# Padding each slot of a weight buffer from 1025 to 1056 elements

## The reference

```python
qkv = xn @ attn_qkvw + attn_qkvb                      # 32 heads of 32
scores = einsum('bhqd,bhkd->bhqk', q, k) * hd ** -0.5
ctx = softmax(scores) @ v;  attn = ctx @ attn_ow + attn_ob

q = xn @ Wq_w.T;  scores = q @ keys.T                 # router, 64 experts
gate = softmax over the top 16 of 64, zero elsewhere
z = (xn @ A_w.T) * gate (each gate for 8 columns)     # 512 columns
out = (z @ B_w.T) * 2
```

## Time and profile before

| | us |
|---|---|
| three timed runs, median | 2559.98 |
| lowest and highest of them | 2558.9, 2560.48 |
| the profiled execution: its time | 2557.13 |
| the profiled execution: its span | 2555.3 |
| TensorE busy in the span | 2507.6 |
| VectorE, ScalarE, GpSimd busy | 1510.5, 1208.0, 1634.3 |

### The profile page before, as it was taken

The page is one execution under the profiler, slowest core; times in us unless marked ns, Lnnn a source line. Parts: engine busy times, 40 slices in busy tenths (PEclk is TensorE's granted clock), DMA queues, the critical chain, the costliest instruction groups (busy, mean ns, idle before and its releaser), DMA issues. The chain is left out here.

```text
span 2555.3 us, 34397 instructions
## 1 busy us (share of the span) xinstructions
PE 2507.6 (98%) x12888; PEld 1633.1 (64%) x12888; DVE 1510.5 (59%) x2524; ACT 1208.0 (47%) x2295; POOL 1634.3 (64%) x556
## 2 busy tenths in 40 slices
PE   7999999999989999999999999999999999989999
PEld 6888887888845555555555555555555555547887
DVE  8511111012668888878888888878878888622221
ACT  2211111110036666766767666666767666761000
POOL 0101111221158999999999999999999999962111
PEclk9999999999989999999999999999999999999999
DMA  4233235423266777787787787787787787664332
GB/s 165 91 124 113 103 113 163 125 74 109 72 169 136 165 158 151 166 164 145 165 166 149 161 166 153 156 166 156 153 169 151 155 169 151 124 159 141 107 108 89
DMA packets 174685, 359.23 MB, mean 141 GB/s; under 512 B 90384, under 2 KB 115472, under 8 KB 143504
## 3 DMA queue, kind: packets, MB, share of 16 engines
q0 software_dynamic: 22752, 165.69, 32.8%
q1 hardware_dynamic: 151792, 191.70, 26.4%
HBM read 127.42 MB, written 63.70 MB: 75 GB/s over the span
## 5 line engine op out<-in xcount | busy, mean ns | idle before, releaser
L1108 DVE TENSOR_REDUCE part_max<-ps_b 128x1 f32<-128x512 f32 x1984 | 1213.7, 679 | 274.6 <-PE ps_b L981 274.2
L932 POOL TENSOR_TENSOR psum_p<-psum_p,probs 128x2048 f32<-128x2048 f32 x253 | 1181.7, 4671 | 53.3 <-ACT probs L1094 43.2
L1094 ACT ACTIVATE probs<-ps_b 128x512 f32<-128x512 f32 x1920 | 970.9, 621 | 357.5 <-PE ps_b L971 354.6
L971 PE MATMUL ps_b<-qp,kp 97*128 97x512 f32 x1344 | 548.0, 413 | 0.0
L981 PE MATMUL ps_b<-kp,qp 96*128 96x512 f32 x1344 | 536.7, 401 | 6.8 <-DMA qp<-qk_scr 6.3
L999 PE MATMUL ps_b<-probs,vh 128*32 128x512 f32 x3840 | 464.4, 598 | 0.5 <-ACT probs L1094 0.5
L971 PEld LDWEIGHTS ps_b<-qp,kp 97*128 97x128 f32 x1344 | 252.3, 188 | 224.3 <-issue 135.8
L320 POOL TENSOR_TENSOR wlo<-wraw,whi 128x1024 fp32r<-128x1024 f32 x21 | 50.3, 2399 | 427.4 <-ACT whi L461 427.4
L971 PE MATMUL ps_b<-qk 97*128 97x512 f32 x704 | 290.4, 416 | 5.3 <-PEq L81 5.2
L981 PEld LDWEIGHTS ps_b<-kp,qp 96*128 96x128 f32 x1344 | 256.9, 191 | 55.5 <-DVE part_max L1108 17.3
L981 PE MATMUL ps_b<-qk 96*128 96x512 f32 x640 | 254.5, 398 | 0.0
(11 more groups left out here) (107 smaller groups left out, 2442.1 us busy)
## 6 DMA issues: line engine op xcount, KB each, us to landing
psum_q<-probs POOLq DMA_DIRECT2D x158, 1024.0 KB, 7.8
qk<-qk_scr SPq DMA_DIRECT2D x66, 256.0 KB, 7.3
qk_scr<-ehi SPq DMA_DIRECT2D x16, 1024.0 KB, 3.9
qk_scr<-elo SPq DMA_DIRECT2D x16, 1024.0 KB, 6.7
kp<-qk_scr SPq DMA_DIRECT2D x63, 256.0 KB, 4.2
qp<-qk_scr SPq DMA_DIRECT2D x63, 256.0 KB, 7.9
wraw<-wcat SPq DMA_DIRECT2D x21, 512.5 KB, 7.5
craw<-cz_scr SPq DMA_DIRECT2D x14, 768.0 KB, 4.9
```

Source lines behind the costliest of these rows:

```text
L932: pool.tensor_tensor(acc[:, :], first[:, :], tile(h, t)[:, :], ALU.add).then_inc(pool_done, 1)
L971: pe.matmul(ps[:, st_bank(n), :], kp[s][0:PACK + 1, t * P:(t + 1) * P], qp[s][0:PACK + 1, b * NQ:(b + 1) * NQ], start=True, stop=True).the ...
L1094: act.activation(tile(h, t)[:, b * NQ:(b + 1) * NQ], ps[:, st_bank(n), :], ACT.Exp, scale=SCALE).then_inc(exp_done, 1)
L1108: dve.tensor_reduce(part_max[hn % 2][:, tn, b:b + 1], ps[:, ring_bank(u), :], AX_X, ALU.max) \
```

## The change

The buffer `wraw` gets slots of 1056 elements in place of 1025; 1056 is the next multiple of 32 above 1025 that the formula gives: (1024 // 32 + 1) * 32. The load writes the first 1025 elements of the slot as before, and all other uses name their elements as before. The last 31 are not used.

```diff
@@ -35,6 +35,7 @@
 WROW = KT * P + 1
+WSLOT = (KT * P // HD + 1) * HD
@@ -87,7 +88,7 @@
-        wraw = sb("wraw", [P, 2, WROW])
+        wraw = sb("wraw", [P, 2, WSLOT])
@@ -215,7 +216,7 @@
             def load_w(blk, slot):
-                sp.dma_start(wraw[:, slot, :], wcat[bass.ds(blk, 1), :, :].rearrange("a p n -> (a p) n")) \
+                sp.dma_start(wraw[:, slot, 0:WROW], wcat[bass.ds(blk, 1), :, :].rearrange("a p n -> (a p) n")) \
                     .then_inc(w_loaded[slot], 16)
```

## The result

| | before | after |
|---|---|---|
| timed runs, median | 2559.44 us (4 runs, 2557.82 to 2560.48) | 2539.52 us (4 runs, 2535.34 to 2542.11) |
| ratio, 95% interval | | 0.9924 [0.9911, 0.9938] |
| profiled execution, time and span | 2557.13, 2555.3 | 2535.34, 2533.5 |

The changed kernel is faster by 0.76%, 19.9 us by the medians. The prediction, 2560.0 us and most probably no change, was wrong, and its range of 2554 to 2564 us didn't hold the time.

A forecast was written before the change was run, and what follows sets the result against it. TensorE, busy 2507.6 of 2555.3 us, was taken as the bound, with projection matmuls every 233.3 ns. Four terms of 0 left the profiled 2557.1 us, 2560.0 us in timed-run terms; range 2554 to 2564 us.

The forecast's parts named there:

- the matmuls' term: Projection stage's 2784 matmuls: interval stays 233.3 ns, change taken as 0, between -35.1 and +3.6 us.
- Its lower bound, from the output projection: Projection matmuls could each gain up to 12.6 ns, as in the output projection's pairs: -35.1 us over 2784.
- the sign of rival 1: Interval between L489's evictions in the projection: 5.30 us would show rival 1, against 5.60 forecast.
- rival 1: Projection matmuls: the 32 bytes keep them from a faster interval; 35 us less, 2525 us; chance 6%.
- What the 32 bytes mean: Projection matmuls: whether an operand starting 32 bytes past a multiple of 128 costs TensorE anything; one nanosecond each is 2.8 us.
- The attention as a control: Attention score matmuls, both operands aligned and new weights each time, run at 234.6 ns; taken as evidence for no gain.
- L429 as a control: First head's score maxima between matmuls of L445: 233.6 ns, three of twelve records aligned; taken as evidence for no gain.
- The output projection: All-aligned matmuls at 227 ns each; the gain was put down to two in a row sharing a stationary operand.
- that wrong split: Output projection pairs: first matmul 233.3 ns, second 220.7, the 12.6 between them read as the price of a new stationary operand.
- The other terms: ScalarE and GpSimd on weights, VectorE, DMAs: each taken as 0; ends -0.4 to +0.4, -0.4 to +0.4, -0.9 to +0.1 us.
- the 1042 that the prediction gave as a sign: ScalarE's rounding of weights would shorten from 1062 to about 1042 ns, without effect on the time.
- places without a term: First 35 us and attention: a change there by more than a microsecond or two would also make the prediction wrong.

The follow-up runs named there:

- experiment 4: Changed kernel with 8 elements of padding ahead of xhi, so xhi, xlo, whi and wlo all start 32 bytes past a multiple of 128: 2543.53 us.
- experiment 1: Kernel before with 96 unused bytes between wraw and whi, wraw's second slot kept at +4: 2554.19 us, ratio 0.9989.
- experiment 5: Kernel without the computation: series of 48 matmuls with operands displaced by various bytes, or partitions varied; 226.8 ns undisplaced, 233.2 with the stationary operand displaced by 32.
- experiment 9: Kernel before with 56 elements ahead of whi: the change's addresses from whi on, wraw's slots not widened: 2536.62 us, ratio 0.9926.
- experiment 11: Kernel without the computation: matmul series at good distances with signals, waits, rotating banks or other engines' work, 226.6 to 227.0 ns; alternating 96 and 97 partitions, 233.6.
- experiment 8: Changed kernel with the new tail and all attention score matmuls over 97 partitions, the added query row zero: 2533.52 us, ratio 0.9925.
- experiment 3: Changed kernel with 8 elements ahead of wlo and 24 behind, so wlo alone is 32 bytes off: 2555.68 us.
- experiment 2: Changed kernel with 8 elements ahead of whi: wraw keeps its new slots, whi and all behind it 32 bytes off again: 2559.6 us, ratio 1.0008.
- the new tail: Product sums_b moved from GpSimd to VectorE, behind its seventh w2lo: kernel before 2552.65 us, changed kernel 2538.31 us.
- experiment 10: Changed kernel with 8 elements ahead of elo: elo, stage, ident and small tensors 32 bytes off again, whi and wlo in place: 2540.68 us.
- experiment 7: Changed kernel rerun, 2539.82 us; with sums_b's product moved from GpSimd to VectorE, kernel before 2552.65 us and changed kernel 2538.31 us.

## Why the prediction was wrong

**The step that failed** is the matmuls' term: "I take 0, the value to which the two cases with new weights each time (L429, the attention) are nearest". Its lower bound, from the output projection, had the right direction. The term measured 6.6 ns a matmul: the quarter takes 5.44 us, where the prediction forecast 5.60 and gave 5.30 as the sign of rival 1. What the runs put in place of each piece:

- *What the 32 bytes mean.* I asked whether an operand that starts 32 bytes past a multiple of 128 costs something. It doesn't (experiment 4), and both at multiples of 128 don't help (experiment 1). The distance between the stationary and the moving operand modulo 256 counts (experiments 4, 5, 9): 32 costs 6.4 ns, 128 costs 5.8, 0 nothing. That L359 and L416 are equally slow fits this as well: between them only the operands' roles are exchanged, so the distance is 32 in one and 224 in the other, for which the series have 233.2 and 233.4 ns.
- *The attention as a control.* Its operands are aligned, but it alternates between 97 and 96 partitions, and that alone gives 233.6 (experiments 5, 11). Without the alternation it still has 231 where 227 would be expected (experiment 8), for a reason that stays open. A control must share everything with the case but the thing asked about, and this one differed in two ways that each hid the effect.
- *L429 as a control.* In the earlier trace rows 9 of the 11 intervals start with a matmul of L445, a displaced one, and one displaced partner in three slows the others too (experiment 3, L84 in experiment 5). The matmuls of 96 partitions between those of 128 cost something of their own as well, as the rows under "The size" show. So 233.6 there says nothing about aligned operands.
- *The output projection.* It was the only clean control: 128 partitions throughout, distances that are multiples of 256, 227 ns. I explained its 6.6 ns away by the stationary operand that two matmuls share, and so split one uniform interval into 233.3 and 220.7. Experiment 5 has 226.8 with new weights for every matmul, and the series that repeats the same operands throughout has 226.9. Sharing a stationary operand gives nothing in this program, where each matmul has a weight load of its own all the same: PEld has 12888 of them, as many as PE has matmuls.

**The size.** Rival 1 was the right case, at 6%. It was sized by the 12.6 ns of that wrong split: -35.1 us. With 233.3 - 226.7 = 6.6 ns x 2784 it would have been 18.4. The two traces show 15.5 of it up to the attention, with 9.6 us in place of 10.8 for the 1632 of the q/k blocks, 4.8 in place of 5.1 for the V stage's 768, and 1.1 in place of 2.5 for the last 384. The 9.6 also hold the clock: the changed kernel's execution had more of it from 25 to 30 us (0.78 against 0.54) and less from 80 to 100 us (0.91 against 1.00). Pairs with like clocks there give more: experiment 2 and the changed kernel (0.91 in both from 80 to 100 us) have their V stages 10.2 us apart and their attentions 16.2, the two kernels with the new tail (0.83 in both) 10.2 and 16.4. Most of the 2 us that are still missing to 18.4 lie in the last 384. In these last blocks matmuls of 96 partitions stand between those of 128. TensorE's timeline after:

```profile
604.57 0.40 PE L430 MATMUL ps_a<-qk 96*128 96x512 f32 x1
604.80 0.40 PE L446 MATMUL ps_a<-xhi,whi 128*128 128x512 f32 x1
...
605.27 0.39 PE L446 MATMUL ps_a<-xhi,wlo 128*128 128x512 f32 x1
...
606.18 0.40 PE L430 MATMUL ps_a<-qk 96*128 96x512 f32 x1
```

The three intervals from L430 on take 0.70 us, 233 each, and the four from 605.27 on 0.91, 227.5 each. The change of the number of partitions costs them 6 ns, as in experiment 5.

**The other terms** held. ScalarE's rounding takes 1.06 us after as before (a median of 1061 ns; the 1042 that the prediction gave as a sign did not come); the loads of wraw let it start 7.5 to 7.6 us after their issue; TensorE's longest waits for others from 35 to 700 us are 1.1 and 0.9 us, against 0.8 and 0.9; the places of elo, stage and the small tensors (experiment 10) and of wraw's slots (experiments 2, 9) count for nothing. The prediction also named the first 35 us and the attention as places without a term. The first 35 us did differ: TensorE's second quarter starts at 34.51 us in place of 35.77, mostly by the higher granted clock. The larger surprise is in the tail: 6.3 us between the two profiles that belong to GpSimd's product.

**The size at like clocks.** The five profiles with a distance of 32 or 128 start the attention at 714.96 to 720.95 us and the ten with a multiple of 256 at 700.87 to 705.06; the means of the four with 32 and of the ten are 14.8 us apart. The granted clock from 35 to 130 us sorts the ten: 700.87 at 1.00, five at 701.76 to 702.65 at 0.98, four at 704.28 to 705.06 at 0.96. Of those with whi and wlo both at 32, before (1.00) starts at 717.27, experiment 2 (0.98) at 717.94, the new tail (0.96) at 720.95. At like clocks the change is thus worth 15 to 17 us up to the attention. The timed pairs say 14.3 (new tail) and 16.5 (experiment 9). The rest of the first comparison's 19.9 fits the short product, which came by chance or not (experiment 7).

**What stays open:** why the distance modulo 256 counts at all. That the reads of the weights and of the moving operand meet in the same part of the memory is a guess; the runs show only that it depends on the difference and not on the places. What keeps the attention's intervals at 231 and above with 97 partitions throughout. Why the V stage keeps a part of the gain in experiment 3 and the q/k blocks none. And whether the change has a part in how often GpSimd's product is short.

## What to carry to other kernels

All of this was measured for float32r matmuls of 512 columns. Where a stage is bound by such matmuls back to back, put the stationary and the moving operands of its matmuls a multiple of 256 bytes apart, and keep the number of partitions the same from one matmul to the next. Each was worth 3% of the interval when measured by itself; in this kernel the first gave about 15 us and the second 5, since other things hold the attention too. A change that pads one tensor moves all that lie behind it, so list the distances between partners before and after, not only the alignment of each. And before a neighbour in the trace serves as a control, look for what else it does differently; the one that contradicts you is the one to explain last.

## What the runs showed of the hardware

- The interval of float32r matmuls of 512 columns, at granted clock 1.00, is 226.6 to 226.7 ns at best in the stretches read from these kernels. The Trainium skill (TensorE: Matmul & The Clock Gate, "Wait — 56ns, not 53.3ns?") gives 215.7 ns for 512 columns as measured, 215.8 by its formula, which the prediction weighed beside rival 1. No stretch read here has it.
- It goes by the signed distance modulo 256: the stationary operand displaced by 32, 64, 96, 128, 160, 192 and 224 gives 233.2, 233.4, 234.2, 232.5, 233.4, 229.0 and 233.4 ns; even 4 and 8 bytes give 232.4 and 230.7. The sign shows at 64: the moving operand displaced by 64, a distance of 192, has 229.1, the stationary one 233.4.
- GpSimd's product of 128x512, two operands from SBUF, took 7.7 to 9.1 us in six profiles and 1.7 to 2.1 in four, with the same program or one that differs in padding. In the long case of before it starts at 2289.45, 0.35 us after the start of a series of six VectorE subtractions of 1.15 us each, which ends at 2296.00, and it ends 1.15 us behind that; in the short case VectorE's series is 1.1 us longer (7.99). The Trainium skill (SBUF — State Buffer, "Who interferes with whom") says that a VectorE instruction with two inputs from SBUF contends with a GpSimd instruction that reads there, over a pair of ports which it calls an exclusive lock. The two cases agree with that. In the long one GpSimd's one instruction lasts until a whole series of VectorE's is over.
- The granted clock of the first 35 us was 0.80, 0.85, 0.90, 0.95 or 1.00 in different executions. The attention's start scattered by 4 us among equal intervals, in the order of the clock of the next stretch: with 1.00 from 35 to 130 us it starts at 700.87, with 0.98 at 701.76 to 702.65, with 0.96 at 704.28 to 705.06. In that stretch the clock fell between 80 and 100 us: to 0.91 in the changed kernel's first profile and to 0.83 in the one with the new tail, while TensorE was busy for all 20 us.
